# Rows interleaved over partitions, late scores off TensorE, the last tile in halves and new instruction orders in a gated attention and feed-forward kernel

## The reference

```python
si = einsum('bnd,d->bn', ctx, W[0, :D]); sj = einsum('bnd,d->bn', ctx, W[0, D:])
xij = sigmoid(si[:, :, None] + sj[:, None, :] + b[0])
x = x + tanh(g_xattn) * (0.6 * xij + 0.4 * layernorm(x))
# ffn, on layernorm(x); bitlinear = rmsnorm, 8-bit rounding per row, ternary weights
h = silu(bitlinear(z, w1)) * bitlinear(z, w2)
out = x + tanh(g_ffn) * bitlinear(h, w3)
```

## Time and profile before

| | |
|---|---|
| median of 3 runs | 158.2 us (157.78 to 158.7) |
| span of the profiled execution | 155.3 us |
| what lies around the span, median less span | 2.9 us |
| PE busy | 139.7 us (90%) |
| DVE busy | 117.9 us (76%) |
| ACT busy | 107.3 us (69%) |
| POOL busy | 101.0 us (65%) |
| HBM read, written | 13.89 MB, 4.19 MB |

### The profile page before, as it was taken

How to read it: one execution, slowest core, us unless ns; L and a number is a source line. 1 busy time by engine, 2 the same in 40 slices (tenths; PEclk the granted TensorE clock), 3 DMA queues, 4 the chain that set the end, 5 groups by cost and what they waited for, 6 DMA issues and landing times.

```text
span 155.3 us, 2445 instructions
## 1 busy us (share of the span) xinstructions
PE 139.7 (90%) x743; PEld 76.7 (49%) x743; DVE 117.9 (76%) x180; ACT 107.3 (69%) x177; POOL 101.0 (65%) x155
## 2 busy tenths in 40 slices
PE   0984965798998999999999999999999999999991
PEld 0883854365555455444444444444454444454540
DVE  0338998998889999999979966489579184669441
ACT  3279998979598489967799286532999636772720
POOL 3302617999892791785989985669968999436210
PEclk9999599779999999999999999999999999999999
DMA  4899999999214189733193695453362807654313
GB/s 146 289 406 395 407 402 414 392 364 347 61 38 93 34 168 212 151 62 69 35 199 64 152 113 146 100 104 126 101 160 60 241 9 189 160 97 93 135 74 129
DMA packets 45237, 26.94 MB, mean 173 GB/s; under 512 B 35751, under 2 KB 37800, under 8 KB 45224
## 3 DMA queue, kind: packets, MB, share of 16 engines
q1 hardware_dynamic: 45216, 26.78, 60.9%
q10 hardware_dynamic: 8, 0.00, 0.0%
HBM read 13.89 MB, written 4.19 MB: 116 GB/s over the span
## 4 chain that ended last, share of the span: by engine, by line
PE 72%; DVE 11%; DMA 5%; POOL 4%; issue 3%; ACT 2%; SPq 1%; DVEq 0%; ACTq 0%; POOLq 0%
PE ps L1307 46%; PE ps L1341 24%; DMA raw_room<-in_L_ffn_w_dram 5%; DVE raw L1038 2%; DVE bn L922 2%; ACT w2T L656 1%; DVE w_abs L972 1%; POOL ln_r L440 1%; DVE w3q L1026 1%; DVE c_all L953 1%; DVE w1T L1009 1%; POOL raw L509 1%; DVE x_top L962 1%; PE ps L1290 1%; POOL slope L443 1%
## 5 line engine op out<-in xcount | busy, mean ns | idle before, releaser
L1307 PE MATMUL ps<-w1T,xqT 128*128 128x512 f16 (+1 forms) x192 | 42.3, 372 | 0.0
L1307 PE MATMUL ps<-w2T,xqT 128*128 128x512 f16 (+1 forms) x192 | 40.7, 361 | 1.1 <-ACT w2T L656 0.6
L1341 PE MATMUL ps<-w3T,hqT 128*128 128x512 f16 x176 | 40.1, 379 | 0.0
L1038 DVE SCALAR_TENSOR_TENSOR raw<-ps,deq,raw_room 128x1408 f32<-128x1408 f32 x16 | 26.9, 1683 | 16.6 <-PE ps L1307 11.2
L721 ACT ACTIVATE raw_room<-ps,deq 128x1408 f32<-128x1408 f32 x16 | 22.9, 1432 | 15.9 <-PE ps L1307 15.8
L521 POOL TENSOR_SCALAR hq<-raw,h_scale 128x1408 f16<-128x1408 f32 x15 | 23.8, 1590 | 9.9 <-DVE h_scale L1048 9.6
L1307 PEld LDWEIGHTS ps<-w1T,xqT 128*128 128x128 f16 x192 | 19.2, 100 | 20.6 <-issue 2.2
L1307 PEld LDWEIGHTS ps<-w2T,xqT 128*128 128x128 f16 x192 | 18.6, 98 | 20.9 <-DVE raw L1038 0.8
L1341 PEld LDWEIGHTS ps<-w3T,hqT 128*128 128x128 f16 x176 | 17.2, 98 | 19.3
L1045 DVE TENSOR_REDUCE h_top<-raw 128x1 f32<-128x1409 f32 x16 | 25.8, 1610 | 0.2
L732 ACT ACTIVATE junk<-raw 128x1410 f16<-128x1410 f32 x16 | 21.9, 1372 | 1.5 <-DVE raw L1038 1.3
(11 more groups left out here) (99 smaller groups left out, 173.5 us busy)
## 6 DMA issues: line engine op xcount, KB each, us to landing
c_all<-in_x_dram SPq DMA_DIRECT2D x16, 256.0 KB, 9.5
out_dram<-out_ring SPq DMA_DIRECT2D x16, 256.0 KB, 2.1
raw<-in_L_ffn_w_dram SPq DMA_DIRECT2D x4, 704.0 KB, 11.2
raw_room<-in_L_ffn_w_dram SPq DMA_DIRECT2D x3, 768.0 KB, 8.2
raw<-in_L_ffn_w_dram SPq DMA_DIRECT2D x3, 768.0 KB, 11.7
hq<-in_ctx_dram SPq DMA_DIRECT2D x4, 256.0 KB, 10.2
raw_room<-in_L_ffn_w_dram SPq DMA_DIRECT2D x1, 512.0 KB, 10.3
raw<-in_L_ffn_w_dram SPq DMA_DIRECT2D x1, 512.0 KB, 10.6
```

Source lines behind the costliest of these rows:

```text
L1038: v.scalar_tensor_tensor(out=hid[:, t % HS, 0:H], in0=ps_up[:, 0:H], scalar=deq[:, 1, t:t + 1], in1=gate[:, t % GATES, :], op0=ALU.mult, o ...
L1307: last = m.matmul(bank[:, lo:hi], xqT[:, i % XT, k, :], wT[w][:, k, lo:hi], start=(k == 0), stop=(k == KD - 1))
L1341: last = m.matmul(ps_y[t % 2], hqT[:, t % HT, k, :], w3T[:, :, k, :], start=(k == 0), stop=(k == KH - 1))
```

## The change

1. **Rows.** Tile i of a batch holds the rows 4p + i of it instead of 128 i + p, so that partition p has four neighbouring rows. The context of a batch is then one contiguous run of 2 KB in each partition. `scores_out` and the direct `score` reorder the spread scores to match.
2. **Late scores.** Batches 0 and 1 have their scores as before. For 2 and 3, `ctx_product(n)` (POOL) multiplies the context by both halves of W, `sum_scores(n)` (DVE) sums over 128 and fills `s_half`, `store_sj(n)` (SP) writes sj to DRAM and `spread_sj(n)` (SP) reads it back, broadcast to all partitions. `turn_ctx`, `ctx_out`, `scores`, `half_scores`, `spread_scores` and `scores_out` of 2 and 3 are gone.
3. **w2** is rounded into a contiguous buffer `w2q` (the room of `hqT`); group 1 is done by ACT.
4. **Last tile.** It is rounded by one DVE instruction, transposed by DMA like the others, multiplied in two halves of 256 columns, and finished and stored in halves.
5. **Orders.** The order of every engine's calls is new. Among others `turn_x(2)` and later ones stand among the loads of x on SP, g0 comes behind all of w2's transposes, and g6, u6 and g7 stand ahead of l0.

The core of the diff:

```diff
-    x_t = x.rearrange("b (t p) d -> (b t) p d", p=P)
+    x_rows = x.rearrange("b (p t) d -> b t p d", p=P)
+    x_t = [x_rows[i // TB, i % TB] for i in range(T)]
-    CONV_POOL = [[], [1, 2, 3, 4], [0, 1, 2, 3]]
+    CONV_ACT = [[], [1], []]
+    CONV_POOL = [[], [2, 3, 4], [0, 1, 2, 3]]
+            def store_sj(n):
+                sp.wait_ge(scores_sb, n + 1)
+                sp.dma_start(sj_rows[n].rearrange("(p t) -> p t", p=P),
+                             s_half[:, n, 1, :]).then_inc(sj_stored[n - PRODUCTS], 16)
+            def spread_sj(n):
+                sp.wait_ge(sj_stored[n - PRODUCTS], 16)
+                sp.dma_start(sj_wide[:, n - len(DIRECT), :],
+                             sj_rows[n:n + 1].broadcast_to([P, N])).then_inc(sj_in[n - PRODUCTS], 16)
...
             def turn_h(t):
-                sp.wait_ge(hq_done, t + 1)
+                if t == T - 1:
+                    sp.wait_ge(hq_last, 1)
+                else:
+                    sp.wait_ge(hq_done, t + 1)
+                if t == 0:
+                    sp.wait_ge(wT_ps, NG)
+                if t == 2:
+                    sp.wait_ge(s_summed, len(LATE))
...
+            def ctx_product(n):
+                if n == PRODUCTS:
+                    pool.wait_ge(w_wide_in, 16)
+                    pool.wait_ge(wT_ps, NG)
+                else:
+                    pool.wait_ge(s_summed, n - PRODUCTS)
+                pool.wait_ge(ctx_ld[n], 16)
+                g.tensor_tensor(ctx_w[:, :, :, :], ctx_sb[n].rearrange("p (u t) d -> p u t d", u=1).broadcast_to([P, 2, TB, DC]),
+                                w_wide[:, :, :].rearrange("p u (t d) -> p u t d", t=1).broadcast_to([P, 2, TB, DC]),
+                                ALU.mult).then_inc(ctx_times_w, 1)
...
+            def sum_scores(n):
+                dve.wait_ge(ctx_times_w, n - PRODUCTS + 1)
+                v.tensor_reduce(out=s_sums[:, n, :, :], in_=ctx_w[:, :, :, :], axis=AX_X, op=ALU.add).then_inc(s_summed, 1)
...
+            def finish_half(n):
+                dve.wait_ge(h_deq_done, HGROUP[t] + 1)
+                dve.wait_ge(x1_done, t - BY_DVE + 1)
+                dve.wait_ge(y_ps, t + 1 + n)
+                v.scalar_tensor_tensor(out=out_ring[:, t % OUTS, c], in0=ps_last[n], scalar=h_deq[:, t:t + 1],
+                                       in1=c_all[:, t, c], op0=ALU.mult, op1=ALU.add).then_inc(out_done[t % OUTS], 1)
...
-            dequant_h(8)
+            add_x(10)
+            dequant_h(8)
+            add_mean(15)
```

More of the change, by code:

```diff
@@ L79, in flamingo_gated_ffn @@
     DIRECT = [0]
+    PRODUCTS = 2
+    LATE = [n for n in range(B) if n >= PRODUCTS]
+    HALF = D // 2
     OUT_DVE = [[], [0, 5]]
@@ L1094, in _ @@
             sum_w(1, 0)
-            make_x(1)
+            evac_rows(6)
+            evac_rows(7)
             half_scores(1)
             clip_w1(0)
-            evac_rows(6)
-            max_x(1)
-            stats_x(2)
-            scale_w(1)
-            weight_factor(0)
-            evac_rows(7)
-            conv_w(1, 0)
-            intercept(2)
-            evac_rows(10)
-            clip_w1(1)
-            clip_w1(2)
-            ctx_out(2)
-            sum_w(2, 0)
-            evac_w(1, 0)
@@ L1112, in _ @@
-            conv_w(1, 5)
-            stats_x(3)
-            scale_w(2)
+            clip_w1(1)
+            evac_rows(10)
+            make_x(1)
+            scale_w(1)
+            conv_w(1, 0)
+            stats_x(2)
+            max_x(1)
+            evac_w(1, 0)
+            sum_w(2, 0)
+            conv_w(1, 5)
+            clip_w1(2)
+            stats_x(3)
+            intercept(2)
+            evac_w(1, 5)
+            stats_x(4)
+            make_x(2)
             weight_factor(1)
-            evac_w(1, 5)
@@ L1117, in _ @@
-            weight_factor(2)
-            make_x(2)
-            half_scores(2)
             max_x(2)
             hidden(0)
-            stats_x(4)
+            intercept(3)
             max_h(0)
-            intercept(3)
+            sum_scores(2)
+            hidden(1)
+            scale_w(2)
+            make_x(3)
+            intercept(4)
+            weight_factor(2)
+            max_x(3)
+            hidden(2)
+            max_h(1)
+            make_x(4)
+            hidden(3)
+            max_x(4)
@@ L1125, in _ @@
             clip_w3(0)
+            max_h(2)
+            hidden(4)
             clip_w3(1)
-            hidden(1)
-            make_x(3)
-            max_x(3)
-            half_scores(3)
-            hidden(2)
-            intercept(4)
-            max_h(1)
             clip_w3(2)
-            hidden(3)
+            stats_x(5)
+            hidden(5)
             clip_w3(3)
-            make_x(4)
-            max_x(4)
-            hidden(4)
-            max_h(2)
-            stats_x(5)
             stats_x(6)
@@ L1143, in _ @@
             max_h(3)
-            hidden(5)
+            hidden(6)
             intercept(5)
+            sum_scores(3)
             max_h(4)
             make_x(5)
+            max_x(5)
+            intercept(6)
+            max_h(5)
+            hidden(7)
             stats_x(7)
-            max_x(5)
-            max_h(5)
-            intercept(6)
-            hidden(6)
+            stats_x(8)
             max_h(6)
-            stats_x(8)
             make_x(6)
-            hidden(7)
+            max_h(7)
```

493 lines of the change are left out of this document (251 added, 242 removed).

## The result

The changed kernel took 164.48 us (median of 4 runs, 164.02 to 166.41), the kernel before 158.45 us beside it (157.78 to 160.47): a ratio of 1.045, 95% interval 1.037 to 1.053. It is slower by 4.5% by that ratio, which leaves out runs in a slower state of the chip and so isn't the quotient of the two medians (1.038); 155.6 was forecast. The profiled execution took 164.02 us, with a span of 162.2.

The account below looks back on a forecast made before the run. PE was taken to bound the kernel, DVE second. Terms -3.2 (ramp), +0.4 (u2 to g7), +0.5 (middle), -0.6 and +0.3 (tail) gave -2.6: 158.2 to 155.6 us; range leaving out 2 in 10, 154.0 to 157.6.

Parts of the forecast that it names:

- Contiguous w2 halves I cost at nothing: Ramp: rounding w2 into contiguous halves adds no time, since DVE and POOL write as many elements.
- the sign "at about 149.3": End of the kernel: an observation that would show the forecast right, PE finishing its work at about 149.3 us.
- The 3.2 us: Ramp, up to product u2: u2 comes at 45.2 instead of 48.49; -3.3 worked out, -3.2 us taken.
- the scale at 24.9 to 25.1: Start of the ramp: the scale of w2 stays at 24.9 to 25.1 us, its loads and their order being unchanged.
- My rival of the clock: Ramp: g0 and u0 both run at 1.2 GHz, u2 comes at 46.5; +1.3 us, 156.9 us in all; chance 0.08.
- +0.8 for DVE's waits: From u2 to g7: u3 waits for hidden(2) and u5 for hidden(4), both from DVE; +0.8 us in all.
- Covered, with nothing to spare: Before l0: the last w3 transpose lands near 70 us, just when l0 is due, so no wait.
- The +0.4 at l2: Middle: batch 3's scores delay turn_h(2), landing at 77.4 with l2 due at 77.0; +0.4 us, 0 to 1.5.
- the size I had given for l4: Middle: l4 and g14 each due within 0.5 us of their transposes' landing; 0.1 us added.
- The round trip through DRAM: Middle: storing sj (2.1 us) and reading it back broadcast (at most 3 us) costs nothing, being covered.
- forecast +0.3: Tail behind PE: halves run one after the other, with add_mean(15) late and store(14) between their stores; +0.3 us.
- 2.9 us as constant: Whole kernel: the profiled span lies 2.9 us below the median time, assumed the same after the change.

Follow-up runs that it names:

- e1: Changed kernel with POOL's w2 conversions multiplying by the scale and by 1.0 again, without the minimum; 157.46 us, ratio 0.999 to the kernel before.
- e2: Kernel before with product and minimum in POOL's w2 conversions, still into every other half word; 168.49 us, ratio 1.068.
- e3: Changed kernel with a maximum against -TINY for the minimum in POOL's w2 conversions; 165.27 us, one run.
- e10_before_contig: Kernel before with only the w2 halves written into a contiguous buffer, POOL still using two products; 156.99 us, ratio 0.995.
- e5_turn7: e1 with turn_x(7) ahead of the third w3 transpose on SP and load_ctx(3) moved between turn_x(4) and turn_x(5); 155.71 us, one run.
- e9_turn7_tail: e1 with the edits of e5_turn7 and e7_tail; 156.42 us, ratio 0.994 to the kernel before.
- e4_loads_first: e1 with all loads of x issued ahead of turn_x(2) on SP; 157.02 us, one run.
- e7_tail: e1 with add_mean(15) before dequant_h(8), square_h(15) behind finish(11), and store(14) before store_half(0); 157.87 us, one run.
- e6_all: e1 with the edits of e4_loads_first, e5_turn7, e7_tail and e8_sum_first together; 156.44 us, ratio 0.990 to the kernel before.
- e8_sum_first: e1 with ACT's last sum over w2 ahead of its copy of tile 0's transposed activations; 158.01 us, ratio 1.003 to the kernel before.
- e11_no_sum: e1 with the edits of e4_loads_first, e5_turn7 and e7_tail, without ACT's reordering; 155.47 us, ratio 0.986 to the kernel before.
- e12_quant7: e11_no_sum with POOL's quant_x(7) ahead of quant_h(2); 156.46 us, ratio 0.989 to the kernel before.

## Why the prediction was wrong

**The step that failed** is the sentence "Contiguous w2 halves I cost at nothing: DVE and POOL write as many elements". The lists counted POOL's conversions at the 1.4 us of before, and the instruction's second operation had changed with its destination. What the runs show in its place is 3.7 to 4.3 us for each of the three, which made PE wait 8.1 us for them and put u2 7.5 us behind the forecast. Nothing in the trace of before shows a product with a minimum on POOL, so it was an operation without a row and had to be bounded like the product of two tensors. The sum over profiles comes out so. u2: 52.68 for 45.2, +7.5. From u2 to PE's end: 105.8 for 103.8, +2.0. Behind PE: 3.8 for 3.65, +0.1. Together 9.6 for a span that is 9.5 longer than the forecast 152.7. (By that sum PE is through at 149.05; the sign "at about 149.3" was a slip.) The cost of the pair is shown three times, by taking it out (e1), by adding it to the kernel before (e2) and by another operation in its place (e3).

**The ramp otherwise.** The table has, for each profile, the mean clock in the stretches 16 to 20 and 20 to 24, the scale's time, u2's time, and what lies between the two:

| profile | clock | scale | u2 | between |
|---|---|---|---|---|
| before | 0.63, 1.00 | 24.98 | 48.49 | 23.5 |
| e10_before_contig | 1.00, 1.00 | 25.93 | 48.39 | 22.5 |
| forecast | | 25.0 | 45.2 | 20.2 |
| after | 0.68, 0.90 | 25.19 | 52.68 | 27.5 |
| e5_turn7 | 1.00, 1.00 | 25.47 | 45.62 | 20.2 |
| e9_turn7_tail | 1.00, 1.00 | 25.16 | 45.99 | 20.8 |
| e4_loads_first | 0.57, 1.00 | 25.31 | 46.65 | 21.3 |
| e7_tail | 0.72, 0.85 | 25.79 | 47.34 | 21.6 |
| e6_all (sum first) | 0.80, 0.50 | 25.88 | 46.55 | 20.7 |
| e8_sum_first | 0.50, 0.50 | 26.51 | 46.66 | 20.2 |
| e1_mult | 0.50, 0.50 | 27.34 | 47.48 | 20.1 |
| e11_no_sum | 0.50, 0.50 | 27.30 | 47.46 | 20.2 |
| e12_quant7 | 0.50, 0.50 | 27.41 | 47.58 | 20.2 |

Without the minimum the 20.2 of the forecast came out in five profiles of nine, and 0.5 to 1.4 more in the others. The 3.2 us were there. I had left the scale at 24.9 to 25.1, as its loads and sums don't change. They don't, but in the changed kernels it moves by 2.3 us between executions (25.16 to 27.41), and it is latest where the clock was at 0.50 while w1 was transposed, since ACT's last sum stands behind a copy that waits for PE. The clock isn't all of it: in e10_before_contig the scale came 0.95 later than before, with the clock at 1.00 in both stretches. My rival of the clock looked behind 20 us, at g0 and u0, and not there. How often the late start falls in each kernel wasn't measured, since only one profile of each has rows. It isn't rare: of the eleven profiles of changed kernels five had the clock at 0.50 from 20 to 24.

**From u2 to g7** I had +0.8 for DVE's waits. Where nothing else is late they cost 0.5 (u2 to u6 is 19.5 us in e4 and e11, for eight products of 2.376). In the changed kernel g3 waited 1.20 for DMA besides, and the stretch took 20.5. "Covered, with nothing to spare" was said of w3's last transpose and l0. In the changed kernel g7, which now stands ahead of l0, waited 1.65 and so hid l0's. I had counted what the order moved on DVE, and not that `turn_x(7)` had come behind three DMAs on SP. Freed of that, l0 waits 0.8 to 1.0 (e5, e6, e9, e11), and 0.45 in e12.

**The middle.** The +0.4 at l2 didn't come: it follows u7 at once. Its list was right in order but started from a later PE. In e9 l6, at 103.83, waited 0.47 for its transpose, of the size I had given for l4. The round trip through DRAM was hidden but for 0.3 us on ACT, though both of its terms were too small: the store of sj took 3.1 to 4.4 us to land in the changed kernel (forecast 2.1) and the broadcast read 3.8 to 3.9 (forecast at most 3).

**The tail.** `turn_last` left PE, and the transpose by DMA in its place was hidden, as forecast. Behind PE it is 0.4 more than before, forecast +0.3. Of the two causes named one does nearly all: `store(14)` between the half stores, some 0.8 us, while the wait for `add_mean(15)` cost under 0.1 (e7_tail). Without both, the halves bring 0.4 against before.

**Around the span.** I took 2.9 us as constant, from the median of other executions less one profiled span. The profiled executions since lie 1.8 above their span (the changed one 164.02 less 162.2), a few up to 2.6. So the profiled execution of before probably took about 157.1, some 1 us less than the median. The forecast of 155.6 is the median less 2.6 and doesn't hang on this. But the span came out 9.5 above its forecast and the median 8.9, by this and by the 0.5 that the changed kernel's profiled execution lies below its median.

**What stays open.** After e1_mult the forecast 155.6 still lacks 1.9 us. e11_no_sum, with the waits before g3 and g7 and the tail's orders treated, is 2.0 us below e1_mult by the medians. But the two profiles, whose starts are alike (u2 at 47.46 and 47.48), differ by 1.1 us in the span: 0.8 behind PE and 0.2 between u2 and PE's end, since most of what g7 no longer waits is waited for at l0 and behind l2. The mean clocks speak against a rarer late start as the rest: among executions above 0.96 the mean times are 157.4 us (ten of e1_mult) and 155.5 (five of e11_no_sum). So 0.9 us of the 2.0 has no cause shown; the two ran on different chips. Nor is it shown why e11_no_sum stands before e6_all, whose intervals overlap.

## What to carry to other kernels

Read a diff operand by operand: a changed operation inside an instruction that keeps its line, shape and count is a new operation, and without a row of its own it gets bounds like any other. On a hand-written queue list, beside what an instruction waits for, what it has to pass on that queue: here two transposes by DMA, each behind loads or other transposes, made PE wait 2.9 us, more than the 1.3 of all the waits that I had worked out. An order that frees one wait is worth only what the next wait doesn't take back: of the 1.75 us before g7, 0.8 came out at l2, and 0.3 at PE's end. And where a start depends on an engine whose clock varies between executions, compare stretches from an inner mark (here the scale of w2) and not from the start of the span.

## What the runs showed of the hardware

- On GpSimd a `tensor_scalar` of 128x1024 from float32 to float16 took 1.1 to 2.3 us with two products (1.1 to 1.7 into contiguous half words), 3.7 to 4.3 us with a product and a minimum or a maximum. On VectorE the product with the minimum took 0.76.
- With two products, the same conversion on GpSimd took 1.41 us into every other half word and 1.12 into contiguous ones, at the fastest.
- A transpose by DMA of 128x512 landed in 2.3 us at best and 2.5 in the median of the changed kernel; issued among 256 KB loads of x it took up to 4.9 there and 5.1 in e8. But one at 104.38, with no load near it, took 4.7 too.
- A store of 2 KB (`store_sj`) took 3.1 to 4.4 us to land in the changed kernel, longer than the 2.1 of a 256 KB tile's store, and 2.1 to 2.8 in the four kernels with all loads of x ahead of it.
- The last half store (128 KB) landed in 2.2 us when issued right behind another store, and without one in 1.9, once in 3.3 (e9).
- In kernels whose instructions up to there are the same, the granted clock from 16 to 24 us was at 0.50 throughout in one execution (e1) and at 1.00 in another (e5), and the work that hung on it came up to 2.3 us later.
